# The gate of every tile writes to SBUF, and VectorE's low parts read SBUF

## The reference

```
def ffn(xf):                                   # 512 x 128, D = 128, F = 64, E = 64 experts
    shared = silu(xf @ Ws_up) @ Ws_down
    aff = xf @ centroids.T
    idx = top_k(aff + expert_biases, 8)
    w = sigmoid(aff[idx]);  w = w / (sum(w) + 1e-08)      # cw: weight per row and expert, 0 elsewhere
    h = silu(einsum('td,edf->etf', xf, W_up))
    routed = einsum('etd,te->td', einsum('etf,efd->etd', h, W_down), cw)
    return shared + routed
```

## Time and profile before

| | |
|---|---|
| median of 3 runs | 822.33 us (821.82 to 822.52) |
| the profiled execution | 821.78 us, span 820.0 us |
| PE busy | 805.1 us (98%) |
| DVE busy | 692.7 us (84%) |
| ACT busy | 650.7 us (79%) |
| POOL busy | 408.3 us (50%) |
| granted TensorE clock | 1.000 of full speed |

### The profile page before, as it was taken

How to read it: one execution, slowest core, us unless ns; L and a number is a source line. 1 busy time by engine, 2 the same in 40 slices (tenths; PEclk the granted TensorE clock), 3 DMA queues, 4 the chain that set the end, 5 groups by cost and what they waited for, 6 DMA issues and landing times.

```text
span 820.0 us, 12468 instructions
## 1 busy us (share of the span) xinstructions
PE 805.1 (98%) x3691; PEld 649.5 (79%) x3691; DVE 692.7 (84%) x1451; ACT 650.7 (79%) x1204; POOL 408.3 (50%) x360
## 2 busy tenths in 40 slices
PE   7999999999999999999999999999999999999998
PEld 5778878778888788888888788887888878888786
DVE  7987989888798887988879888798897988788875
ACT  5897778778787787877878688886888868786975
POOL 2884545545455453544535445364463644554453
PEclk9999999999999999999999999999999999999999
DMA  7000000000000000000000000000000000000000
GB/s 267 23 0 14 14 1 1 1 10 17 14 1 0 21 4 13 0 0 26 0 13 0 0 26 0 13 0 0 26 0 0 0 1 27 0 1 1 14 0 14
DMA packets 16046, 11.51 MB, mean 14 GB/s; under 512 B 1680, under 2 KB 14992, under 8 KB 16016
## 3 DMA queue, kind: packets, MB, share of 16 engines
q1 hardware_dynamic: 16016, 11.15, 4.4%
HBM read 9.05 MB, written 2.10 MB: 14 GB/s over the span
## 4 chain that ended last, share of the span: by engine, by line
PE 77%; DVE 14%; ACT 5%; issue 1%; POOL 1%; DMA 0%; DVEq 0%; ACTq 0%; POOLq 0%
PE up L711 12%; PE up L712 12%; PE up L713 12%; PE y_ps L711 11%; PE y_ps L713 11%; PE y_ps L712 11%; PE side L720 3%; DVE x L656 3%; DVE g_lo L589 2%; DVE gated L580 2%; ACT up L421 2%; ACT g_hi L429 2%; DVE normed L526 2%; DVE up L580 2%; PE side L731 1%
## 5 line engine op out<-in xcount | busy, mean ns | idle before, releaser
L353 POOL TENSOR_TENSOR g_lo<-gated,g_hi 128x512 fp32r<-128x512 f32 x256 | 331.9, 1297 | 372.5 <-ACT g_hi L429 372.5
L421 ACT ACTIVATE up<-up 128x512 f32<-128x512 f32 x528 | 310.7, 590 | 73.6 <-PE up L713 72.1
L580 DVE TENSOR_TENSOR gated<-up,cw 128x512 f32<-128x512 f32 x256 | 175.3, 685 | 58.1 <-ACT up L421 53.9
L711 PE MATMUL y_ps<-g_hi,wd_hi 128*128 128x512 f32 x512 | 208.0, 406 | 1.8 <-POOL g_lo L353 1.7
L711 PE MATMUL up<-x_hi,wu_hi 128*128 128x512 f32 x512 | 203.1, 397 | 1.8 <-DVE g_lo L589 1.8
L713 PE MATMUL y_ps<-g_hi,wd_lo 128*128 128x512 f32 x512 | 202.5, 396 | 0.0
L712 PE MATMUL up<-x_lo,wu_hi 128*128 128x512 f32 x512 | 202.3, 395 | 0.0
L713 PE MATMUL up<-x_hi,wu_lo 128*128 128x512 f32 x512 | 201.7, 394 | 0.0
L712 PE MATMUL y_ps<-g_lo,wd_hi 128*128 128x512 f32 x512 | 201.6, 394 | 0.0
L429 ACT CAST g_hi<-up 128x512 fp32r<-128x512 f32 x272 | 161.2, 592 | 47.8 <-DVE up L580 45.8
L580 DVE TENSOR_TENSOR up<-up,cw 128x512 f32<-128x512 f32 x256 | 176.4, 689 | 18.1 <-ACT up L421 14.4
(11 more groups left out here) (101 smaller groups left out, 570.9 us busy)
## 6 DMA issues: line engine op xcount, KB each, us to landing
x_in<-in_x SPq DMA_DIRECT2D x8, 256.0 KB, 2.8
wu_raw<-in_w_up SPq DMA_DIRECT2D x4, 512.0 KB, 6.1
wd_raw<-in_w_down SPq DMA_DIRECT2D x4, 512.0 KB, 7.0
x_res<-in_x SPq DMA_DIRECT2D x8, 256.0 KB, 2.8
out<-out_sb SPq DMA_DIRECT2D x7, 256.0 KB, 2.2
out<-out_sb SPq DMA_DIRECT2D x2, 128.0 KB, 1.9
sm_raw<-in_ident SPq DMA_DIRECT2D x2, 64.0 KB, 5.4
ident<-in_ident SPq DMA_DIRECT2D x1, 64.0 KB, 2.2
```

The lines of the kernel that those rows point to most:

```text
L353: nc.gpsimd.tensor_tensor(g_lo[:, i, :], gated[:, t // 2 % ORING, :], g_hi[:, i, :].bitcast(fp32), ALU.subtract).then_inc(lo_done[1], 1)
L421: nc.scalar.activation(up[i][:, :], up[i][:, :], ACT.Silu).then_inc(silu_done, 1)
L580: nc.vector.tensor_tensor(gated[:, t // 2 % ORING, :] if t % 2 else up[i][:, :], up[i][:, :], cw[ph.q][:, :], ALU.mult).then_inc(gate_done, 1)
L711: nc.tensor.matmul(o, a[0], b[0], start=start, stop=False)
```

## The change

The gate of every tile from 1 to 32 writes to `gated`, which has eight buffers in place of four and is indexed by t in place of t // 2. The high parts of even tiles (ScalarE) and their low parts (VectorE) read `gated`; tile 0 still uses its PSUM bank. `free_bank` waits for the gate of any tile but tile 0. GpSimd's low part only has another index.

```
-ORING = 4
+ORING = 8
...
-                nc.gpsimd.tensor_tensor(g_lo[:, i, :], gated[:, t // 2 % ORING, :], g_hi[:, i, :].bitcast(fp32),
+                nc.gpsimd.tensor_tensor(g_lo[:, i, :], gated[:, t % ORING, :], g_hi[:, i, :].bitcast(fp32),
...
-                src = gated[:, t // 2 % ORING, :] if t % 2 else up[t % RING][:, :]
+                src = gated[:, t % ORING, :] if t > 0 else up[0][:, :]
                 nc.scalar.copy(g_hi[:, t % GRING, :], src).then_inc(hi_done, 1)
...
-                nc.vector.tensor_tensor(gated[:, t // 2 % ORING, :] if t % 2 else up[i][:, :], up[i][:, :], cw[ph.q][:, :],
+                nc.vector.tensor_tensor(gated[:, t % ORING, :], up[i][:, :], cw[ph.q][:, :],
                                         ALU.mult).then_inc(gate_done, 1)
...
-                nc.vector.tensor_tensor(lo[ps, i, :], up[t % RING][ps, :], g_hi[ps, i, :].bitcast(fp32),
+                nc.vector.tensor_tensor(lo[ps, i, :], gated[ps, t % ORING, :] if t > 0 else up[0][ps, :], g_hi[ps, i, :].bitcast(fp32),
                                         ALU.subtract).then_inc(lo_done[0], 1)
...
-                if tile % 2:
+                if tile > 0:
                     pe.wait_ge(gate_done, NJ * (ph.p - back) + tile)
                 else:
                     pe.wait_ge(lo_done[0], low_count(ph, t))
```

## The result

The changed kernel takes 830.68 us (830.66 to 830.84, 4 runs) against 822.08 us (821.73 to 822.52, 4 runs) of the kernel before, measured beside it: ratio 1.0106, 95% interval 1.0092 to 1.012. It is 8.6 us slower. 824.4 us was forecast, with a range that ended at 829.0.

The account below looks back on a forecast made before the run. TensorE, busy 98% of the span, was taken as the bound. Terms 0 - 0 + 1.5 + 0.5 = 2.0 us on the profiled 821.78 gave 823.8; the run median's 0.55 offset made 824.4 us, range 820.3 to 829.0.

Parts of the forecast that it names:

- The bank frees: Even tiles' banks free at the gate; at most 3.4 us of up-product waits saved, taken as 0 because ScalarE's copy stays late.
- The operands: ScalarE's SBUF reads add 5.9 us over its span, 0 on the path; undisturbed VectorE low parts cost 0 more.
- the 0.75 to 0.8 us that was named: Sign in the changed kernel's trace: VectorE's low parts with a mean of some 0.75 to 0.8 us, not 681 ns.
- Tile 17 of pass A: GpSimd's low part of tile 17 comes late, TensorE waits 0.3 us in each of five passes: 1.5 us.
- The low part of tile 32 beside rstd: Sign: VectorE's low part of tile 32 takes 0.69 us beside rstd, against GpSimd holding the interface through rstd.
- the second rival: GpSimd's rstd also holds the interface, delaying tile 32's low part and the copy: 3.3 us more, 827.7 us; chance 0.10.
- Pass B: Tile 14's low part delays rstd and then the norms by up to 0.5 us; counted 0, upper end 3.5 us.
- First pass: At tile 21, VectorE's low part of tile 20 pushes GpSimd's full queue back: 0.5 us on the path.
- The rival of piled-up collisions: In bursts each delayed low part delays the next gate; a fifth of 67 us reaches TensorE: 13 us, 835; chance 0.10.
- Delays in the first pass fall into the bank waits that are gone: First-pass delays ahead of tile 21's push were taken to be absorbed by the removed bank waits, with no cost.

Follow-up runs that it names:

- the run with two banks: The kernel before with eight buffers, only even tiles 30 and 32 (not in the first pass) going through SBUF, ScalarE's copy unmoved: 822.08 us.
- the experiment with two tiles: The changed kernel with tile 14 (steady table B passes) and tile 16 (table A passes) going through their PSUM bank as before: 826.61 us.
- late banks: The changed kernel with even tiles' banks again freed at their low part instead of at the gate: 835.78 us.

## Why the prediction was wrong

**Right.** The bank frees bring nothing by themselves in the steady passes, since the copy does not come earlier: the earlier trace rows against the rows of ScalarE above, and the run with two banks (822.08). The operands cost next to nothing by themselves (0.5 us, or none). VectorE's low parts have a mean of 781 ns, inside the 0.75 to 0.8 us that was named. Tile 17 of pass A was put at 0.3 us and measured 0.27 by the distances of matmul starts (0.14 to 0.16 ahead of the first matmul, 0.11 ahead of the second). The low part of tile 32 beside rstd took 0.69 us, so the second rival falls:

```profile
476.19 1.04 POOL L343 TENSOR_TENSOR rstd<-var_eps,neg_half 128x4 f32<-128x4 f32 x1
```
```profile
476.51 0.69 DVE L589 TENSOR_TENSOR g_lo<-gated,g_hi 128x512 fp32r<-128x512 f32 x1 [0.69 <-ACT g_hi L429]
```

The reason given beside it, that a short VectorE instruction passes, is wrong. In the kernel before `w_eps`, 0.15 us beside rstd, took 1.07 us when it was issued at 402.44 inside a GpSimd low part (402.19 to 403.49). It is GpSimd's instruction, rstd with four elements a partition, that lets VectorE pass.

**Wrong, the size of two terms.** *Pass B* was counted at 0, on the ground that no matmul after the first pass waited for a GpSimd low part. That ground looked at the wrong consumer: rstd's delay goes to the norms, and to transposes. The upper end that was given, 0.5 us a pass, is what came, 0.46 in each of five passes and 0.4 in pass 2, 2.7 us in all. *First pass* was counted as one push of 0.5 us at tile 21. The trace has a push at each low part while GpSimd's queue is full, and the delayed low parts wait in turn; 2.93 us by the table, and 2.5 less when it was undone (6.1 us over the kernel before, against 8.6). The remaining passes were not looked at: 0.92 in pass 1, where the wait for norms grew by 0.91, and 0.47 in the last. So the sum was 1.5 + 0.5 = 2.0, where the table has 3.8 for passes 3 to 12, 2.9 for the first and 2.3 for the others, 9.0 in all (spans: 828.9 - 820.0 = 8.9). By cause, 2.7 are the norms, 1.4 (5 x 0.27) tile 17, 2.9 the first pass and 0.9 pass 1; some 1.1 are not placed.

The rival of piled-up collisions took a share of 67 us of random meetings. Its mechanism, each delayed low part delaying what follows, is at work in the first pass. VectorE's stretched low parts came to 25.7 us, and the experiment with two tiles shows that in the steady passes it isn't a pile but two instructions.

**Wrong in the other direction.** "Delays in the first pass fall into the bank waits that are gone" put the use of the early frees in the wrong place. The first pass is as long with late banks; but in pass 2 and the passes B they save 1.2 to 1.3 us each, and over the span 5.4 us, which no term of the sum had. They bring no time alone and save much once low parts are late.

## What to carry to other kernels

Price a new contention at the instructions without slack, and follow the engine that is held up to every consumer (here norms and transposes), not only to the one that the edit touches. A wait that is removed pays only if the next one does not stand on a chain of its own; look there. Two banks freed early brought 0, the copy moved ahead of an instruction that idles brought 1.7 us, and both together 4.9. To relieve an operand or a bank, change only the tiles that need it: with two of sixteen even tiles changed the bank waits of the later passes were gone, and no loss showed.

## What the runs showed of the hardware

VectorE's low part with two SBUF operands and a GpSimd instruction of 512 elements a partition exclude each other whichever comes first: beside one it took 1.18 to 1.48 us for 0.68, and GpSimd's took 1.74 for 1.29 (all of GpSimd's here read SBUF; one that only writes was not tried). Two large operands are not needed for it. The norms, which read one tensor from SBUF and two numbers a row, and `w_eps`, with four elements, wait in the same way (two norms 1.39 us beside a GpSimd low part, where four take 1.11; `w_eps` 1.07 for 0.15). The low parts with one operand in PSUM (681 ns in the mean) and the gates (0.65 to 0.70 us, all 512) never did.

A GpSimd instruction with four elements a partition keeps VectorE out only briefly: a low part issued 0.10 us into rstd took 0.67 us (81.74 against 81.64 in the changed kernel), and one issued 0.32 us into it took 0.69, both undisturbed, while the reverse order, 0.04 us apart, cost rstd 0.49 us (1.53 for 1.04). So which of the two is issued first decides, within 0.14 us here, whether half a microsecond is lost. Nearer than 0.10 us behind rstd no low part was seen.
